# Statistics on two engines, a projection by pairs of rows, a store on another queue, and inputs loaded one stage ahead

## The reference

```python
def _L0(x):                          # 16 channels in z
    a = sigmoid((x @ Wa1 + ba1) * (x @ Wa2 + ba2))
    b = sigmoid((x @ Wb1 + bb1) * (x @ Wb2 + bb2))
    g = sigmoid(x @ Wg + bg)
    z = einsum('bikc,bkjc->bijc', a, b)
    return g * (_ln(z, ln2_g, ln2_b) @ Wz + bz)
def _L1(x, mask):                    # 64 channels in y
    xn = _layernorm(x, ln1_w, ln1_b)
    h = (xn @ pi_w.T + pi_b) * sigmoid(xn @ gi_w.T + gi_b) * mask[..., None]
    a1, b1, a2, b2 = split(h, 4, axis=-1)
    y = concat([einsum('bikd,bjkd->bijd', a1, b1), einsum('bkid,bkjd->bijd', a2, b2)], -1)
    yn = _layernorm(y, ln2_w, ln2_b)
    return (yn @ po_w.T + po_b) * sigmoid(yn @ go_w.T + go_b)
x1 = x + _L0(_gn(x), ...)
out = x1 + _L1(_gn(x1), ...)
```

## Time and profile before

| | before |
|---|---|
| median of 3 runs | 4955.36 us (4944.73 to 4981.35) |
| profiled execution | 4947.65 us, its span 4945.9 us |
| mean granted TensorE clock | 0.975 of full speed |
| PE, DVE busy | 4032.7 us (82%), 4055.3 us (82%) |
| ACT, POOL busy | 3362.1 us (68%), 2672.1 us (54%) |
| HBM read, written | 1009.59 MB, 522.19 MB, 310 GB/s over the span |

### The profile page before, as it was taken

How to read it: one execution, slowest core, us unless ns; L and a number is a source line. 1 busy time by engine, 2 the same in 40 slices (tenths; PEclk the granted TensorE clock), 3 DMA queues, 4 the chain that set the end, 5 groups by cost and what they waited for, 6 DMA issues and landing times. The chain is left out here.

```text
span 4945.9 us, 90448 instructions
## 1 busy us (share of the span) xinstructions
PE 4032.7 (82%) x26438; PEld 2225.3 (45%) x26438; DVE 4055.3 (82%) x5836; ACT 3362.1 (68%) x4752; POOL 2672.1 (54%) x1428
## 2 busy tenths in 40 slices
PE   0004898794699999969999999979999987888888
PEld 0002555452355555535555555545554433444444
DVE  4888888778788887779999999967779997777777
ACT  0004999754577777658888888856667776888887
POOL 0000000085577777747777777763324426888887
PEclk9999999997799999979999999999999998999999
DMA  7996889653999999969998898876668859999999
GB/s 273 369 382 255 319 321 331 238 175 118 297 360 367 361 355 347 340 227 310 314 313 307 313 314 311 311 248 227 229 229 296 303 207 346 407 404 403 403 403 365
DMA packets 700450, 1532.72 MB, mean 310 GB/s; under 512 B 32800, under 2 KB 50656, under 8 KB 697952
## 3 DMA queue, kind: packets, MB, share of 16 engines
q1 hardware_dynamic: 632800, 1397.68, 79.9%
q10 hardware_dynamic: 67584, 134.23, 7.0%
HBM read 1009.59 MB, written 522.19 MB: 310 GB/s over the span
## 5 line engine op out<-in xcount | busy, mean ns | idle before, releaser
L1654 POOL TENSOR_TENSOR s_oT<-s_gated,s_x1t 128x1024 f32<-128x1024 f32 x256 | 689.2, 2697 | 222.9 <-DVE s_gated L1573 217.9
L888 POOL TENSOR_TENSOR s_x1T<-s_gz,s_xT 128x512 f32<-128x512 f32 x512 | 651.5, 1273 | 204.1 <-DVE s_gz L854 202.2
L1029 POOL TENSOR_TENSOR s_low<-s_xc,s_high 128x1024 f16<-128x1024 f32 x256 | 547.6, 2139 | 257.2 <-ACT s_high L992 257.1
L1331 PE MATMUL s_y_ps<-s_ab 128*128 128x512 f16 x3072 | 678.4, 379 | 1.8 <-DVE s_ab L1402 1.8
L795 PE MATMUL s_g_ps<-s_xT,s_Wg 128*128 128x512 f32 x1024 | 523.8, 593 | 0.0
L854 DVE SCALAR_TENSOR_TENSOR s_gz<-s_z_ps,k_z_bias,s_g 128x512 f32<-128x512 f32 x512 | 384.5, 751 | 164.3 <-ACT s_g L821 162.1
L634 POOL MEMSET s_total<- 128x2048 f32 x1 | 1.8, 1809 | 956.4 <-POOLq L41 956.4
L821 ACT ACTIVATE s_g<-s_g_ps,s_bg 128x512 f32<-128x512 f32 x512 | 352.0, 687 | 191.4 <-PE s_g_ps L795 191.4
L1573 DVE SCALAR_TENSOR_TENSOR s_gated<-s_p_ps,k_po_bias,s_gate 128x1024 f32<-128x1024 f32 x256 | 328.7, 1284 | 178.8 <-ACT s_gate L1610 156.0
L1331 PEld LDWEIGHTS s_y_ps<-s_ab 128*128 128x128 f16 x3072 | 300.5, 98 | 343.4 <-issue 2.1
L468 DVE SCALAR_TENSOR_TENSOR s_low<-s_x_ps,k_gn_scale,s_high 128x512 f16<-128x512 f32 x512 | 359.8, 744 | 89.0 <-ACT s_high L425 88.4
(11 more groups left out here) (216 smaller groups left out, 9458.2 us busy)
## 6 DMA issues: line engine op xcount, KB each, us to landing
s_xt<-in_x SPq DMA_DIRECT2D x128, 1024.0 KB, 6.9
s_xt<-in_x SPq DMA_DIRECT2D x256, 512.0 KB
x_d<-s_x1T SPq DMA_DIRECT2D x128, 1024.0 KB, 8.7
s_xt<-x_d SPq DMA_DIRECT2D x128, 1024.0 KB, 9.3
h_d<-s_h SPq DMA_DIRECT2D x128, 1024.0 KB, 6.5
s_x1t<-x_d SPq DMA_DIRECT2D x128, 1024.0 KB, 14.1
out<-s_ot ACTq DMA_DIRECT2D x128, 1024.0 KB, 9.3
s_mask_b<-mask_d SPq DMA_DIRECT2D x128, 512.0 KB, 4.4
```

Source lines behind the costliest of these rows:

```text
L888: pool.tensor_tensor(x1T[:, i // U, i % U, :], gz[:, i % 4, :], xT[:, i % 8, :], ALU.add).then_inc(added, 1)
L1029: pool.tensor_tensor(low[:, n % 4, :, :], xc[:, n % 4, :, :], high[:, n % 4, :, :], ALU.subtract).then_inc(rest_ready, 1)
L1331: last = pe.matmul(y_ps[:, ib, 0:N], ab[:, u % 2, 0, a, kb, ib * P:(ib + 1) * P], ab[:, u % 2, 1, b, kb, :], start=m == 0, stop=m == len(t ...
L1654: pool.tensor_tensor(oT[:, n % 4, :, :], gated[:, n % 4, :, :], x1t[:, n // 2, 2 * (n % 2):2 * (n % 2) + 2, :], ALU.add).then_inc(added, 1)
```

## The change

1. `prepare`: the 45 weight loads are dealt to SP and ACT in turn; SP then issues the first two chunks of x (into stage 1's buffers), ahead of the wait for the weights. `prepare` runs inside stage 1.
2. Stage 1: ACT takes 6 of the 32 groups of 4 channels, with two ACTIVATE (Identity and Square, 128x512) each that sum as they go; the DVE keeps 26, and adds a reduce, a scale and two copies at the end. SP then loads the first 6 groups of stage 2.
3. Stage 2: 6 groups in a pass; `turn` takes two rows (8 transposes) at a time, `x_ps` has three slots of two banks; `round_high` and `rest` take two rows at once (128x1024); `p_ps` has one bank per factor; a sigmoid is taken once before the loop.
4. Stage 4: the store of x1 is issued by ACT instead of SP. When the loop is done, SP loads the first 8 tiles of x1 for stage 5.
5. Stage 5: the variance on the DVE is gone, ACT's root reads the statistics with bias and scale; a sigmoid is taken once before the loop. The first loads of x1 are those of 4.
6. Stage 6: SP loads the first 4 tiles of x1 for stage 7 at its end, which stage 7 no longer loads.

```diff
+                for dst, src in loads[0::2]:
                     sp.dma_start(dst, src).then_inc(loaded, 16)
+                load_ahead(sp)
                 sp.wait_ge(loaded, 16 * len(loads))
+
+            @block.scalar
+            def _(act):
+                for dst, src in loads[1::2]:
+                    act.dma_start(dst, src).then_inc(loaded, 16)
...
             def _(sp):
-                with sp.Fori(0, chunks // 2) as r:
+                with sp.Fori(0, chunks // 2 - 1) as r:
                     for u in range(2):
                         sp.wait_ge(used, r * 2 + (u + 1))
-                        sp.dma_start(xt[:, u, :, :], x_v[bass.ds(r * 2 + u, 1)].rearrange("a p t c -> p (a t) c")).then_inc(loaded[u], 16)
+                        sp.wait_ge(summed, r * 2 + (u + 1))
+                        load(sp, r + 1, u)
+                for k in range(ahead.GROUPS):
+                    ahead.load(sp, 0, k)
...
+                def chunk(r, u):
+                    act.wait_ge(loaded[u], r * 16 + 16)
+                    if not isinstance(r, int) or r or u:
+                        act.wait_ge(summed, r * 2 + u)
+                    for g in range(BY_ACT):
+                        for m, func in enumerate((ACT.Identity, ACT.Square)):
+                            last = act.activation(unused[m][:, g, :].rearrange("p (t c) -> p t c", c=4),
+                                                  xt[:, u, :, 4 * (BY_DVE + g):4 * (BY_DVE + g) + 4], func,
+                                                  accum_out=sums[:, m, g, bass.ds(r * 2 + u, 1)])
+                    last.then_inc(summed, 1)
...
-                def turn(r, g, j):
-
-                    if j == 0:
-                        pe.wait_ge(loaded[g % GROUPS], (r + g // GROUPS) * 16 + 16)
-                    pe.wait_ge(rest_ready, r * BODY + (U * g + j + 1))
-                    for q in range(CB):
-                        last = pe.transpose(x_ps[:, j, q * P:(q + 1) * P], xt[:, g % GROUPS, j, q, :], K.ident[:])
+                pe.sem_inc(done, 2 * GROUPS)
+
+                def turn(r, g, h):
+
+                    k, n = g % GROUPS, (2 * g + h) % SLOTS
+                    if h == 0:
+                        pe.wait_ge(loaded[k], (r + g // GROUPS) * 16 + 16)
+                    pe.wait_ge(rest_ready, r * PAIRS + (2 * g + h + 1))
+                    for j in range(2):
+                        for q in range(CB):
+                            last = pe.transpose(x_ps[:, n, j, q * P:(q + 1) * P], xt[:, k, 2 * h + j, q, :], K.ident[:])
                     last.then_inc(turned, 1)
 
                 def product(r, g, m):
-                    pe.wait_ge(rest_ready, r * BODY + (U * g + U + U))
-                    pe.wait_ge(gated, r * GROUPS + (g + 1))
+                    pe.wait_ge(rest_ready, r * PAIRS + (2 * g + 2 + SLOTS))
+                    if m == 0:
+                        pe.wait_ge(opened, r * GROUPS + (g + 1))
+                    else:
+                        pe.wait_ge(gated, r * GROUPS + (g + 2))
...
-                def step(r, g, last=False):
-                    for j in range(U):
-                        if not (last and g + 2 >= GROUPS):
-                            turn(r, g + 2, j)
-                        if j % 2 == 1 and not (last and g + 1 >= GROUPS):
-                            product(r, g + 1, j // 2)
+                def step(r, g, end=None):
+                    for h in range(2):
+                        if end is None or g + 2 < end:
+                            turn(r, g + 2, h)
+                        if end is None or g + 1 < end:
+                            product(r, g + 1, h)
...
-                def round_high(r, g, j):
-                    act.wait_ge(turned, r * BODY + (U * g + j + 1))
-                    if j == 0:
-                        act.wait_ge(done, r * (2 * GROUPS) + (2 * g + 2))
-                    act.activation(high[:, g % 4, j, :], x_ps[:, j, 0:N], ACT.Copy, scale=K.gn_scale[:]).then_inc(rounded, 1)
+                act.sem_inc(opened, 1)
+
+                def round_high(r, g, h):
+                    act.wait_ge(turned, r * PAIRS + (2 * g + h + 1))
+                    if h == 0:
+                        act.wait_ge(done, r * PAIRS + (2 * g + 2))
+                    act.activation(high[:, g % GROUPS, 2 * h:2 * h + 2, :], x_ps[:, (2 * g + h) % SLOTS, :, 0:N], ACT.Copy,
+                                   scale=K.gn_scale[:]).then_inc(rounded, 1)
...
-                def step(r, g, last=False):
-                    for j in range(U):
-                        if not (last and g + 2 >= GROUPS):
-                            round_high(r, g + 2, j)
-                        if j == 1 and not (last and g + 1 >= GROUPS):
-                            open_first(r, g + 1)
+                    if k % 3 == 0:
+                        act.wait_ge(stored[k // 3], (r + g // GROUPS) * 16 + 16)
+                    act.activation(ab[:, k // 3, k % 3, :], gate[:, g % 2, :], ACT.Sigmoid).then_inc(sig, 1)
+
+                def step(r, g, end=None):
                     sigmoid(r, g)
+                    if end is None or g + 3 < end:
+                        round_high(r, g + 3, 0)
+                    if end is None or g + 2 < end:
+                        open_first(r, g + 2)
+                    if end is None or g + 3 < end:
+                        round_high(r, g + 3, 1)
...
+                act.activation(bias_gate[:], K.bg[:], ACT.Sigmoid)
...
-                def group(r, n, last=False):
-
-                    sp.wait_ge(added, r * ROWS + (U * n + U + 8))
-                    sp.dma_start(x1_d[bass.ds(r * ROWS + U * n, U)].rearrange("i p j -> p i j"), x1T[:, n, :, :]).then_inc(stored[n], 16)
-                    if not last:
-                        sp.wait_ge(turned, r * ROWS + (U * n + U))
-                        load_x(r + 1, n)
-                        sp.wait_ge(z_prod, r * ROWS + (U * n + U))
-                        load_z(r + 1, n)
+                def group(r, n):
+
+                    sp.wait_ge(turned, r * ROWS + (U * n + U))
+                    load_x(r + 1, n)
+                    sp.wait_ge(z_prod, r * ROWS + (U * n + U))
...
-                    group(N // ROWS - 1, n, last=True)
+                    sp.wait_ge(stored[n], ahead.BODY // ROWS * 16 + 16)
+                for k in range(ahead.GROUPS):
+                    ahead.load(sp, 0, k)
...
+                def store(r, n):
+                    act.wait_ge(added, r * ROWS + (U * n + U + 8))
+                    act.dma_start(x1_d[bass.ds(r * ROWS + U * n, U)].rearrange("i p j -> p i j"), x1T[:, n, :, :]).then_inc(stored[n], 16)
+
+                def step(r, i, first=False, last=False):
                     act.wait_ge(g_prod, r * ROWS + (i + 1))
                     act.activation(g[:, i % 2, :], g_ps[:, i % 2, 0:N], ACT.Sigmoid, bias=bg[:]).then_inc(sig, 1)
                     if not (last and i + 4 >= ROWS):
                         keep(r, i + 4)
-
+                    if i % U == 2 and i > U:
+                        store(r, i // U - 1)
+                    elif i % U == 2 and not first:
+                        store(r - 1, GROUPS - 1)
 
                 act.activation(g[:, 0, 0:1], K.bg[:], ACT.Sigmoid)
...
                 def deviation(r, b):
-                    act.wait_ge(chain, r * 6 + (3 * b + 1))
-                    act.activation(dev[:], var[:], ACT.Sqrt).then_inc(dev_ready, 1)
+                    act.wait_ge(counted, r * BODY + (16 * b + 18))
+                    if not (isinstance(r, int) and r + b == 0):
+                        act.wait_ge(chain, r * 4 + 2 * b)
+                    spreads = stats[:, b % 2, :, :, :, :].rearrange("p t n a (e k) -> p (t n a e) k", k=3)
+                    act.activation(dev[:], spreads[:, :, 2], ACT.Sqrt, bias=eps[:], scale=1.0 / P).then_inc(dev_ready, 1)
...
+                act.activation(unused[:], K.bg[:], ACT.Sigmoid)
...
-                def variance(r, b):
-                    dve.wait_ge(counted, r * BODY + (16 * b + 18))
-                    spreads = stats[:, b % 2, :, :, :, :].rearrange("p t n a (e k) -> p (t n a e) k", k=3)
-                    dve.scalar_tensor_tensor(var[:], spreads[:, :, 2], 1.0 / P, eps[:], ALU.mult, ALU.add).then_inc(chain, 1)
...
+                for k in range(ahead.GROUPS):
+                    ahead.load(sp, 0, k)
```

More of the change, by code:

```diff
@@ L413, in _ @@
                         step(r, g)
-                for g in range(GROUPS):
-                    step(REPS - 1, g, last=True)
+                for g in range(TAIL):
+                    step(REPS - 1, g, TAIL)
             @block.scalar
@@ L476, in multiply, with step @@
                                              ALU.add, ALU.mult).then_inc(gated, 1)
[L478 to L483 removed]
+                def step(r, g, end=None):
+                    multiply(r, g)
+                    if end is None or g + 2 < end:
+                        for h in range(2):
+                            rest(r, g + 2, h)
@@ L828, in _ @@
```

(4 more changed lines are left out.)

264 lines of the change are left out of this document (155 added, 109 removed).

## The result

| | before | after |
|---|---|---|
| median | 4967.28 us (4944.73 to 4981.35) | 4825.53 us (4822.65 to 4827.47) |
| ratio | | 0.9718, 95% interval 0.9675 to 0.9762 |
| profiled execution's span | 4945.9 us | 4825.7 us |
| mean granted TensorE clock | 0.975 | 0.975 |
| ACT, DVE busy | 3362.1, 4055.3 us | 3395.2, 3925.1 us |

The account below looks back on a forecast made before the run. It took the transfer to bound stage 1, ACT stage 2, PE at full DMA stage 4, the DVE stage 5 and DMA stage 7. Terms -45 + 42 + 0 - 9 - 24 - 8 + 2 = -42 on 4947.65 gave 4906 us, range 4822 to 4938.

Parts of the forecast that it names:

- Stage 2: Stage 2 term: product, transposes, rounding, remainder and handoffs take 4.40 us a group, 563 us against 521, so +42 us.
- Stage 4: Stage 4 term: moving the store to ACT's queue lets x load earlier, worth 0; bounds -76 and +76 us.
- earlier issue helps only if the DMA engines were ever idle, and they are full at 1.04: Stage 4 step: with no idle DMA engines, issuing x sooner gains nothing, so the term was 0.
- what is slow is the packets in the dips beside each z load: Stage 4 step: the lost DMA rate was laid to z's loads, whose rows lie 512 KB apart.
- Rival B: Stage 4: two queues carry the data better, PE's pace binds, 76 us less, 4830 us in all or up to 4870; chance 0.33.
- Rival D: Stage 4: x goes ahead of z, z lands later and PE waits; 4982 us if the loss doubles; chance 0.12.
- Prepare and stage 1: Start and stage 1: earlier first chunk at 36.9, chunks 21.45 us apart at 391 GB/s, shorter tail; -45 us together.
- Stage 4 to 5: Between stages 4 and 5: early x1 loads remove most of ACT's 10.39 us wait at its first affine; -9 us.
- Stage 5: Stage 5 term: -18 us from table waits at pass heads, -6 from the variance at 0.2 us a block; sum -24.
- Stage 7: Stage 6 to 7 term: four x1 tiles, 4.2 MB, load early, 10.6 us of full DMA; taken as -8 us.

Follow-up runs that it names:

- s2_order: Changed kernel with both pairs of a group transposed ahead of the products and both ACT roundings ahead of the first factor's copy; ratio 0.9514 to the kernel before.
- s4_held: Changed kernel, store of x1 still on ACT, but SP's load of x waits for its group's sums; ratio 0.9759 to the kernel before, stage 4 at 770.6 us.
- s4_z_packed: Changed kernel with stage 4's store back on SP and z read from consecutive addresses; ratio 0.9859 to the kernel before, stage 4 at 887.9 us.
- s4_mixed_split: Changed kernel with even groups' store and load of x on SP, odd groups' on ACT, z on SP; ratio 1.0108 to the kernel before, stage 4 945.7 us.
- s4_undone: Changed kernel with stage 4's store of x1 back on SP, ahead of the loads of x and z; ratio 0.9904 to the kernel before, stage 4 at 829.7 us.
- s5_variance: Changed kernel with stage 5's variance on the DVE again; ratio 0.9723 to the kernel before, stage 5 at 1041.5 us against 1043.4.
- s4_swapped: Changed kernel with all of stage 4's stores on SP and all its loads on ACT; ratio 0.9814 to the kernel before, stage 4 at 819.4 us.

## Why the prediction was right or wrong

- **Stage 2** (+42, measured +43.6): right, link by link. The chain was a cost of the order, not of the larger tiles: s2_order keeps the tiles and takes 437.1 us.
- **Stage 4** (0, measured -75.7): wrong, and the main part of the 78 us that were missed. The step that failed is "earlier issue helps only if the DMA engines were ever idle, and they are full at 1.04", from which the term was put at 0. Earlier issue indeed did nothing (s4_held), but a full share is not a full rate: at shares of 1.03 to 1.05 the eleven kernels' windows moved 318 to 391 GB/s. With the store moved to ACT the stage moved 391 instead of 358, and PE's pace bounded it. The step under it failed too, "what is slow is the packets in the dips beside each z load": the dip follows the store, and z's rows do not make it (s4_z_packed).
- **Rival B** had the place, the row of stage 7 for it and the full price (-76, to PE's pace); it got 0.33, because I laid the slow packets to z. Its reason, that two queues carry the stage better, is half right: s4_mixed_split has two queues and is slower than one. The rule cited from the Trainium skill (DMA: Bandwidth & Descriptors, "Issuing engines are not separate DMA queues") gives a term of 0; the runs disagree. With x held behind the sums in both, and only the store issued by another engine, the stage moved 390 GB/s (s4_held) against 365 (s4_undone), and the measurement decides.
- **Rival D** (x ahead of z makes z late) did not occur: PE was busy in all of stage 4's window.
- **Prepare and stage 1** (-45, measured -63.3): the first chunk came as forecast; the pace was mis-sized. I took 391 GB/s from a window that holds the dip in which chunk 1 landed (at 62.68; in 60 to 64 the engines were busy 0.81 and moved 295 GB/s). With the buffer free after 15.5 us the stage moves 414, 20.18 us a chunk: ((355.77 - 15.53) - 37.50) / 15. Fifteen times 1.27 us is 19 us, and 18.3 were missed.
- **Stage 4 to 5** (-9, measured -8.8): right.
- **Stage 5** (-24, measured -13.1): mis-sized. The variance was worth nothing (s5_variance), as the row of ACT's table load said, and even the 0.2 us a block were too much. The pass heads did lose their waits, 20.0 us before and 2.5 after, but in the same place the DVE now waits 30.5 us for PE instead of 18.8. The line of h in stage 5, before and after:

```profile
L1102 DVE SCALAR_TENSOR_TENSOR s_h<-s_p_ps,k_pi_bias,s_gate 128x1024 f32<-128x1024 f32 x255 | 326.4, 1280 | 52.3 <-ACT s_gate L997 20.0 <-PE s_p_ps L1173 18.8
```

```profile
L1201 DVE SCALAR_TENSOR_TENSOR s_h<-s_p_ps,k_pi_bias,s_gate 128x1024 f32<-128x1024 f32 x255 | 326.9, 1282 | 45.2 <-PE s_p_ps L1268 30.5 <-ACT s_gate L1099 2.5
```

- **Stage 7** (-8, measured -3.5): r still had to come. Its first matmul waits for it as long as before, 30.37 and 30.26 us:

```profile
4096.42 1.03 PE L1512 MATMUL s_r_ps<-s_rt,k_halves 4*128 4x512 f16 x2 [30.37 <-DMA s_rt<-r_d]
```

```profile
3979.70 1.03 PE L1620 MATMUL s_r_ps<-s_rt,k_halves 4*128 4x512 f16 x2 [30.26 <-DMA s_rt<-r_d]
```

  A full DMA with 4.2 MB less is worth a third of the 10.6 us here.
- **The total.** That 4825.5 lies within 5 us of rival B's 4830 is in part luck: beside stage 4, the 18.3 us more in stage 1 and what stages 2, 5 and 7 fell short (1.6, 10.9 and 4.5) nearly cancel.

## What to carry to other kernels

Read a stage's DMA by its GB/s beside its share: full engines at 350 GB/s where another stage gets 400 may have something to give. Here it came with moving the stores to ACT's queue, without loads. Two queues are not enough for it (s4_mixed_split), and neither are stores and loads apart (s4_swapped), so try the assignment and the order of issue rather than trust a rule. After widening tiles follow the chain from the last consumer back through each engine's order, since each link grows by a whole tile: the sum of four rows gave the stage to 1%, and showed which two lines to exchange for another 120 us. A removed instruction is worth what the next releaser allows, and nothing if that one was due anyway (s5_variance).
